# Delta rule in a decoder: one wide product with the block inverse in place of two narrow passes

## The chip, the cores and the metric

The program runs on one NeuronCore of one Trainium2 chip. The metric is the device time of one execution in microseconds; the median of three runs is given. Differences of about 0.3% are what a measurement of this kernel can tell from no change.

## What is computed

The reference is a small decoder of two layers on x of shape (8, 128, 256). The change lies in the attention of the second layer, a gated delta rule with 16 key heads and 32 value heads of width 128. After the projections, a causal convolution over 4 taps and silu, it does this for each of 32 heads and 8 batches:

```python
g = -jnp.exp(A_log) * jax.nn.softplus(a + dt_bias)
gc = jnp.cumsum(gT.reshape(Bs, NV, N, CHUNK), axis=-1)
diff = gc[..., :, None] - gc[..., None, :]
decay = jnp.exp(jnp.where(tril, diff, 0.0)) * tril
A = -(jnp.einsum('bhnid,bhnjd->bhnij', k_beta, kc) * decay) * strict
Tm = jax.scipy.linalg.solve_triangular(eye - A, eye, lower=True, unit_diagonal=True)
u = jnp.einsum('bhnij,bhnjv->bhniv', Tm, v_beta)
...
attn = jnp.einsum('bhid,bhjd->bhij', q_i, k_i) * dec_i
v_new = u_i - jnp.einsum('bhid,bhdv->bhiv', kcd_i, St)
out_i = inter + jnp.einsum('bhij,bhjv->bhiv', attn, v_new)
```

The result is normalised by its root mean square, gated with silu(z) and multiplied by W_out. The kernel takes a sequence of 128 as one chunk, which gives the same numbers: it solves one triangular system of 128 rows for each head and batch, and multiplies the solution by the decayed matrix of queries and keys.

## The kernel before

The program has four phases, one after the other: "a" and "b" are layer 0, "c" is the delta rule, "d" is the rest of layer 1. Names in the profile carry the phase, so `c_NP` is the tile NP of the delta rule. Only phase c is touched.

Phase c works in 8 rounds of 4 value heads (2 key heads) and 8 batches, 32 items of 128x128 each. Rounds 0 to 6 are an iteration of a loop each and prepare the next round inside themselves (`more` is true); round 7 stands behind the loop and prepares nothing. A round does this, in the order written out by hand for each engine:

- SyncE (`gather`) has brought the four 32x32 diagonal blocks of every item's key matrix into the tile A and has cleared them in NP. NP holds for each item two 128x128 matrices side by side: index 0 is N, the decayed key matrix, index 1 is the decayed query matrix, here called Q.
- VectorE inverts the diagonal blocks in 62 steps on the tile T (L1549 to L1553) and then copies T with its indices exchanged into A (L1554). `scatter` on SyncE stores T and A to HBM and loads them as block diagonals into Tb and TbT (L1069 to L1077). Meanwhile TensorE projects the four value chunks (L1172, `c_wv`) and the output gate z (L1232).
- VectorE convolves (L1501), ScalarE applies silu (L1385), TensorE transposes the values (L1221).
- The **products pass**: 32 items Tb x N in `items("MT_ps", ...)`, copied by ScalarE over N, four items of 128 columns in a copy (`c_NP<-c_bank`). The transposes of value chunks 2 and 3 stand between them, each behind the silu of its chunk.
- Three **apply passes** of 32 items: Y = V - M Y, VectorE subtracts (L1566). ScalarE and VectorE prepare the next round's four key and query chunks meanwhile; of each chunk ScalarE makes the square (L1390), whose column sums TensorE takes with a one-column matmul for each batch (`norms`, L1182). VectorE adds a convolution tap after each of the last three subtractions of a pass, and convolves the fourth chunk after the third pass.
- The **W pass**: 32 items TbT x Y, copied by ScalarE back to Y.
- `norms` of the third chunk, then the **C pass**: 32 items Q x W, copied by ScalarE to Y and squared by ScalarE (L1442) and GpSimd (L1131) for the root mean square.
- `norms` of the fourth chunk, then decays and gram matrices of the next round, and the output projection (L1326).

All engines take their instructions in order. PSUM has 8 banks; passes over items take banks 0 to 3 in turn, so group n waits for the copy of group n - 4. A float32 matmul is two hardware instructions with a weight load each, so 32 items are 64 matmuls in the trace.

Of the kernel before, what the change touches and what calls it, by code (L numbers as in the profile page):

```python
# [10 lines left out]
F32 = mybir.dt.float32  # L11
# [7 lines left out]
P = 128  # L19
# [34 lines left out]
class Phase:  # L54
# [5 lines left out]
    def sb(self, name, shape, dt=F32):  # L60
        return self.ctx.enter_context(self.nc.sbuf_tensor(f"{self.tag}_{name}", shape, dt))
# [880 lines left out]
HB = 4  # L942
# [12 lines left out]
def layer1_delta_rule(nc, sems, d, x_src, x_dst):  # L955
# [7 lines left out]
    with ctx:  # L963
# [38 lines left out]
        Tb = sb("Tb", [P, ITEMS, P])  # L1002
        TbT = sb("TbT", [P, ITEMS, P])
        Y = sb("Y", [P, HB, B, S])
# [5 lines left out]
        HALF_ITEMS = ITEMS // KB  # L1010
        blocks = nc.dram_tensor("diagonal_blocks", (3, NBL, ITEMS, BL, BL), F32, kind="Internal").ap()
        no_blocks = nc.dram_tensor("no_blocks", (BL, ITEMS, BL), F32, kind="Internal").ap()
        names = """none_stored blocks_out T_out A_out weights consts pool_step x_loaded xT_ps xT_copied ba_ps gate_step gate_act gc_ps gates_ready
            qk_loaded v_loaded z_loaded out_loaded gates_used proj_ready pad_ready tap0_ready conv_step cv_ready silu_ready sq_ready norms_ps
            root_ready rms_ready csqa_ready norm_step gcrow_ps E_ready GP_ps NP_ready gathered elim_step Tb_placed TbT_placed diag_cleared
            vt_ps V_ready z_ps z_ready MT_ps MT_ready apply_ps y_ready W_ps W_ready C_ps C_ready csq_ready s2_ready
            var_ready f_step y_scaled yT_ps yT_ready out_ps acc_step
            ln_step ln_log ln_rstd xo_ready stored""".split()
        s = {n: sem(n) for n in names}
        quads = [(h, q) for h in range(HB) for q in range(2)]  # L1020
        flat = lambda ap: ap.rearrange("p a b -> p (a b)")
        ELIM = 2 * (BL - 1) + 2
        BLOCKS_OUT = 16 * KB * NBL
# [13 lines left out]
        def _(sp):  # L1037
# [29 lines left out]
            def scatter(i):  # L1067

                sp.wait_ge(s["elim_step"], at(i, ELIM, ELIM - 1))  # L1069
                sp.dma_start(blocks[1].rearrange("r t i j -> (r t) i j"), T[:, :, :]).then_inc(s["T_out"], 16)  # L1070
                sp.wait_ge(s["elim_step"], at(i, ELIM, ELIM))
                sp.dma_start(blocks[2].rearrange("r t i j -> (r t) i j"), A[:, :, :]).then_inc(s["A_out"], 16)
                for n, dst, out, placed in ((1, Tb, "T_out", "Tb_placed"), (2, TbT, "A_out", "TbT_placed")):
                    sp.wait_ge(s[out], at(i, 16, 16))
                    for r in range(NBL):
                        rows = slice(BL * r, BL * r + BL)
                        sp.dma_start(dst[rows, :, rows], blocks[n, r].rearrange("t i j -> i t j")).then_inc(s[placed], 16)  # L1077

# [29 lines left out]
        def _(pool):  # L1108
# [13 lines left out]
            link(pool.memset(Tb[:, :, :], 0.0))  # L1122
            link(pool.memset(TbT[:, :, :], 0.0))
            link(pool.memset(pad[:, :, :, :], 0.0))
# [12 lines left out]
        def _(pe):  # L1137
# [86 lines left out]
            def out_gate(i, b):  # L1224
# [8 lines left out]
                last.then_inc(s["z_ps"], 1)  # L1233

            def items(ps, n, lhsT, rhs):

                h, q = quads[n]
                for b in range(4):
                    last = pe.matmul(banks[n % 4][:, b * P:(b + 1) * P], lhsT(h, 4 * q + b), rhs(h, 4 * q + b), start=True, stop=True)  # L1239
                last.then_inc(s[ps], 1)  # L1240

            def apply(i, rep):

                y = V if rep == 0 else Y
                for n in range(8):
                    if rep == 0:
                        pe.wait_ge(s["MT_ready"], at(i, 8, min(n + 5, 8)))
                    else:
                        pe.wait_ge(s["y_ready"], at(i, 24, 8 * (rep - 1) + n + 1))
                    if n >= 4 or rep:  # L1250
                        pe.wait_ge(s["y_ready"], at(i, 24, 8 * rep + n - 3))
                    items("apply_ps", n, lambda h, b: NP[:, h, b, 0, :], lambda h, b: y[:, h, b, :])
# [7 lines left out]
            def round_(i, more):  # L1260
# [10 lines left out]
                pe.wait_ge(s["pad_ready"], at(i, 2 * CHUNKS, 2 * CHUNKS))  # L1271
                for n in range(8):
                    if n >= 4:
                        pe.wait_ge(s["MT_ready"], at(i, 8, n - 3))
                    items("MT_ps", n, lambda h, b: Tb[:, h * B + b, :], lambda h, b: NP[:, h, b, 0, :])
                    if n == 2:
                        values(i, 2)
                    if n == 6:
                        values(i, 3)
# [11 lines left out]
                if more:  # L1291
                    norms(i + 1, 1)
                pe.wait_ge(s["TbT_placed"], at(i, 16 * NBL, 16 * NBL))
                for n in range(8):
                    pe.wait_ge(s["y_ready"], at(i, 24, 16 + max(n + 1, min(n + 5, 8))))
                    if n >= 4:
                        pe.wait_ge(s["W_ready"], at(i, 8, n - 3))
                    items("W_ps", n, lambda h, b: TbT[:, h * B + b, :], lambda h, b: Y[:, h, b, :])
                if more:
                    norms(i + 1, 2)  # L1300
                for n in range(8):
                    pe.wait_ge(s["W_ready"], at(i, 8, min(n + 5, 8)))
                    if n >= 4:
                        pe.wait_ge(s["C_ready"], at(i, 8, n - 3))
                    items("C_ps", n, lambda h, b: NP[:, h, b, 1, :], lambda h, b: Y[:, h, b, :])
# [38 lines left out]
        def _(act):  # L1344
# [68 lines left out]
            def round_(i, more):  # L1413
# [7 lines left out]
                copy_in(i, QK + 3)  # L1421
                for n, (h, q) in enumerate(quads):
                    if n == 2:
                        silu(i, QK + 2)
                    if n == 3 and more:
                        copy_in(i + 1, 0)
                    if n == 5:
                        silu(i, QK + 3)
                    copy_quad(i, "MT_ps", n, NP[:, h, 4 * q:4 * q + 4, 0, :], "MT_ready")
                if more:  # L1430
# [44 lines left out]
        def _(dve):  # L1475
# [67 lines left out]
            def round_(i, more):  # L1543
# [5 lines left out]
                for j in range(BL - 1):  # L1549
# [600 lines left out]
```

## Time and profile before

| | |
|---|---|
| median of 3 runs | 2425.04 us (2422.2 to 2428.43) |
| the profiled execution | 2429.71 us |
| its span in the profile | 2428.0 us |
| mean granted TensorE clock | 0.891 |
| TensorE matmul busy | 2050.6 us, 84% |
| VectorE busy | 1460.7 us, 60% |
| ScalarE busy | 880.9 us, 36% |
| GpSimd busy | 140.1 us, 6% |

The share of busy time says that TensorE matters most. Matmuls overlap in this count, so a busy TensorE may still have room. What a change is worth is read from the stretch that it touches, instruction by instruction, and from the wait that ends last there.

### The profile page before, as it was taken

To read this page: it belongs to the slowest core of one execution; us is meant where nothing else is said; L and a number is where in the kernel's file an instruction comes from. 1 tells how busy PE (TensorE), PEld (TensorE's weight loads), DVE (VectorE), ACT (ScalarE), POOL (GpSimd) and SP (SyncE) were. 2 spreads that over 40 slices of the span, in tenths; PEclk is the share of its full clock that TensorE was granted. 3 is DMA by queue.
4 is the path that set the end of the run, shared out by engine and by line. 5 is a ranking of instruction groups with operands and counts; after the bars stand their busy time and mean duration, and the time that the engine had idled before them with its cause. 6 is when DMAs were issued, how large, how long until landed. Compare 5 with 4: busy or idle time off the path is not lost. (4 is left out here: it accounts for less than half of the span.)

```text
span 2428.0 us, 30948 instructions
## 1 busy us (share of the span) xinstructions
PE 2050.6 (84%) x10836; PEld 1521.5 (63%) x10850; DVE 1460.7 (60%) x3251; ACT 880.9 (36%) x1542; POOL 140.1 (6%) x130
## 2 busy tenths in 40 slices
PE   6988987998985889898998989989899883787786
PEld 4867776554553568485684856848668582465454
DVE  3557665323222576767767667676676854657666
ACT  2433433111113445443453534535345431333233
POOL 1011010000002000000000000000000001011110
PEclk8889888999996889999999999999999995787787
DMA  3000000400001120301203012030120202000000
GB/s 125 5 13 9 4 5 24 165 1 9 0 9 56 36 53 19 77 9 36 53 19 79 10 36 53 14 81 11 36 53 14 66 1 68 7 11 9 10 4 5
DMA packets 163244, 78.53 MB, mean 32 GB/s; under 512 B 140530, under 2 KB 152628, under 8 KB 162132
## 3 DMA queue, kind: packets, MB, share of 16 engines
q1 hardware_dynamic: 163124, 76.99, 11.7%
q8 instruction: 68, 1.11, 0.2%
q14 instruction: 52, 0.43, 0.1%
HBM read 59.88 MB, written 16.91 MB: 32 GB/s over the span
## 5 line engine op out<-in xcount | busy, mean ns | idle before, releaser
L1566 DVE TENSOR_TENSOR c_Y<-c_V,c_bank 128x512 f32<-128x512 f32 x192 | 131.9, 687 | 82.2 <-PE c_bank L1239 82.2
L1239 PE MATMUL c_bank<-c_Y,c_NP 128*128 128x128 f32 x1536 | 176.4, 276 | 0.0
L1239 PEld LDWEIGHTS c_bank<-c_Y,c_NP 128*128 128x128 f32 x1536 | 173.9, 192 | 3.3 <-issue 3.3
L1540 DVE SCALAR_TENSOR_TENSOR c_NP<-c_NP,c_cj,c_bank 128x256 f32<-128x256 f32 x256 | 104.9, 476 | 68.5 <-ACT c_NP L1410 68.5
L1172 PE MATMUL c_bank<-c_xT,c_wv 128*128 128x512 f32 x256 | 123.1, 643 | 26.9 <-issue 23.3
L1172 PE MATMUL c_bank<-c_xT,c_wqk 128*128 128x512 f32 x256 | 128.6, 650 | 5.1 <-ACT c_pad L1366 3.1
L1501 DVE SCALAR_TENSOR_TENSOR c_cv<-c_pad,c_wcqk,c_cv 128x1024 f32<-128x1024 f32 x96 | 122.2, 1280 | 12.2 <-ACT c_cv L1380 11.4
L1501 DVE SCALAR_TENSOR_TENSOR c_cv<-c_pad,c_wcv,c_cv 128x1024 f32<-128x1024 f32 x96 | 122.5, 1283 | 4.8 <-ACT c_cv L1380 1.6
L1326 PE MATMUL c_bank<-c_wout,c_yT 128*128 128x256 f32 x512 | 121.3, 383 | 0.0
L1366 ACT ACTIVATE c_pad<-c_bank 128x512 f32<-128x512 f32 x128 | 69.0, 592 | 131.7 <-PE c_bank L1172 131.7
L1172 PEld LDWEIGHTS c_bank<-c_xT,c_wv 128*128 128x128 f32 x256 | 52.2, 207 | 94.4 <-issue 94.1
L1232 PE MATMUL c_bank<-c_wz,c_xT 128*128 128x512 f32 x256 | 111.2, 592 | 0.0
L855 ACT ACTIVATE b_sg<-b_G 128x512 f32<-128x512 f32 x50 | 29.8, 597 | 220.6 <-PE b_G L808 220.6
L901 DVE TENSOR_TENSOR b_inner<-b_prod,b_R 128x512 f32<-128x512 f32 x44 | 30.3, 688 | 125.8 <-PE b_R L822 88.2
L1410 ACT ACTIVATE c_NP<-c_bank,c_gcnR 128x128 f32<-128x128 f32 x256 | 73.2, 368 | 84.6 <-PE c_bank L1195 84.5
L1131 POOL TENSOR_TENSOR c_V<-c_Y 128x512 f32<-128x512 f32 x32 | 33.3, 1041 | 1199.5 <-ACT c_Y L1403 1199.5
L1326 PEld LDWEIGHTS c_bank<-c_wout,c_yT 128*128 128x128 f32 x512 | 93.9, 192 | 10.9 <-ACT c_yT L1454 0.2
L808 PE MATMUL b_G<-b_xT,b_wup 128*128 x200 | 97.3, 610 | 2.0 <-ACT b_partsT L858 2.0
L808 PE MATMUL b_U<-b_xT,b_wup 128*128 x200 | 94.6, 595 | 0.0
L832 PE MATMUL b_Y<-b_wdown,b_inner 128*128 128x256 f32 x400 | 93.8, 379 | 0.6
L1552 DVE TENSOR_TENSOR c_tmp<-c_A,c_T 128x31 f32<-128x31 f32 (+15 forms) x248 | 84.9, 342 | 15.0 <-DMA c_A<-diagonal_blocks 6.0
L1385 ACT ACTIVATE c_qkT<-c_cv 128x1024 f32<-128x1024 f32 x32 | 34.0, 1062 | 161.9 <-DVE c_cv L1501 161.9
(409 smaller groups left out, 4262.3 us busy)
## 6 DMA issues: line engine op xcount, KB each, us to landing
b_wup<-b_in_wup SPq DMA_DIRECT2D x4, 1280.0 KB, 14.3
c_wqk<-c_in_wqk SPq DMA_DIRECT2D x9, 512.0 KB, 3.4
c_wv<-c_in_wv SPq DMA_DIRECT2D x8, 512.0 KB, 3.4
c_wz<-c_in_wz SPq DMA_DIRECT2D x8, 512.0 KB, 5.6
c_wout<-c_in_wout SPq DMA_DIRECT2D x8, 512.0 KB, 4.5
diagonal_blocks<-c_NP SPq DMA_DIRECT2D x64, 64.0 KB
c_A<-diagonal_blocks SPq DMA_DIRECT2D x8, 512.0 KB, 3.5
c_NP<-no_blocks SPq DMA_DIRECT2D x32, 128.0 KB, 3.8
```

The costliest lines, as they stand in the source:

```text
L808: last = pe.matmul(bank[:, :], wup[:, t, k, m, :], xT[:, bass.ds(i, 1), m, :].rearrange("p a n -> p (a n)"), start=m == 0, stop=m == DC - 1)
L832: last = pe.matmul(Y[b // 2][:, b % 2 * D:(b % 2 + 1) * D], inner[:, n % 2, b * P:(b + 1) * P], wdown[:, n, :], start=False, stop=n == ECH ...
L1172: last = pe.matmul(four(pair[q][:, :]), w[:, c * P:(c + 1) * P], xT[:, c, 4 * q:4 * q + 4, :], start=c == 0, stop=c == DC - 1)
L1232: last = pe.matmul(banks[6 + b % 2][:, :], xT[:, c, b, :], wz[:, c, :], start=c == 0, stop=c == DC - 1)
L1239: last = pe.matmul(banks[n % 4][:, b * P:(b + 1) * P], lhsT(h, 4 * q + b), rhs(h, 4 * q + b), start=True, stop=True)
L1326: last = pe.matmul(banks[2 + m % 2][:, 0:D], yT[:, m % 2, h, :], wout[:, h, :], start=h == 0, stop=h == HB - 1)
L1366: act.activation(pad[:, m % 2, 4 * q:4 * q + 4, TAPS - 1:], four(pair[q][:, :]), ACT.Copy)\
L1410: act.activation(NP[:, h, 4 * q + b, 1, :], banks[4 + n % 2][:, b * P:(b + 1) * P], ACT.Exp, bias=gcnR[:, h, 4 * q + b:4 * q + b + 1]).the ...
L1501: dve.scalar_tensor_tensor(cv[:, m % 2], pad[:, m % 2, :, t:t + S], w, cv[:, m % 2], ALU.mult, ALU.add)\
L1540: dve.scalar_tensor_tensor(NP[:, h, bb, :, :], spread(NP[:, h, bb, 1, :], 2), cj[:, h, bb:bb + 1], gp, ALU.mult, ALU.mult).then_inc(s["NP_ ...
L1552: elim(dve.tensor_tensor(part, along(A[:, j, j + 1:BL], w), spread(T[:, j, 0:w], n), ALU.mult))
L1566: dve.tensor_tensor(rr(Y, h, q), rr(V, h, q), four(banks[n % 4][:, :]), ALU.subtract).then_inc(s["y_ready"], 1)
```

## The change

N and Q of an item lie side by side in NP. The changed kernel multiplies both by the block inverse in one matmul of 256 columns, Tb x [N Q], and copies both products back over NP. The C pass then takes Y itself, since (Tb Q) transposed times Y is what Q transposed times the W pass's result was. The W pass, its copies, the tile TbT, its memset on GpSimd, the exchanged copy of T on VectorE and five DMAs of `scatter` go. In `products` a unit is two items in one bank; 16 units with a copy of 512 columns each take the place of 8 groups of four items. The C pass waits for the third pass's subtractions (`y_ready`) as the W pass did. `silu(i + 1, 3)` of ScalarE moves from between the W copies to behind the second C copy.

```diff
-                sp.wait_ge(s["elim_step"], at(i, ELIM, ELIM))
-                sp.dma_start(blocks[2].rearrange("r t i j -> (r t) i j"), A[:, :, :]).then_inc(s["A_out"], 16)
-                for n, dst, out, placed in ((1, Tb, "T_out", "Tb_placed"), (2, TbT, "A_out", "TbT_placed")):
...
-            link(pool.memset(TbT[:, :, :], 0.0))
...
+            def products(i, u):
+
+                h, b0 = units[u]
+                if u >= 4:
+                    pe.wait_ge(s["MT_ready"], at(i, UNITS, u - 3))
+                for b in range(2):
+                    last = pe.matmul(banks[u % 4][:, b * 2 * P:(b + 1) * 2 * P], Tb[:, h * B + b0 + b, :],
+                                     NP[:, h, b0 + b, :, :].rearrange("p a n -> p (a n)"), start=True, stop=True)
+                last.then_inc(s["MT_ps"], 1)
...
-                for n in range(8):
-                    if n >= 4:
-                        pe.wait_ge(s["MT_ready"], at(i, 8, n - 3))
-                    items("MT_ps", n, lambda h, b: Tb[:, h * B + b, :], lambda h, b: NP[:, h, b, 0, :])
-                    if n == 2:
+                for u in range(UNITS):
+                    products(i, u)
+                    if u == 5:
                         values(i, 2)
-                    if n == 6:
+                    if u == 13:
                         values(i, 3)
...
                 apply(i, 2)
                 if more:
                     norms(i + 1, 1)
-                pe.wait_ge(s["TbT_placed"], at(i, 16 * NBL, 16 * NBL))
-                for n in range(8):
-                    pe.wait_ge(s["y_ready"], at(i, 24, 16 + max(n + 1, min(n + 5, 8))))
-                    if n >= 4:
-                        pe.wait_ge(s["W_ready"], at(i, 8, n - 3))
-                    items("W_ps", n, lambda h, b: TbT[:, h * B + b, :], lambda h, b: Y[:, h, b, :])
                 if more:
                     norms(i + 1, 2)
                 for n in range(8):
-                    pe.wait_ge(s["W_ready"], at(i, 8, min(n + 5, 8)))
+                    pe.wait_ge(s["y_ready"], at(i, 24, 16 + max(n + 1, min(n + 5, 8))))
...
-                for n, (h, q) in enumerate(quads):
-                    if n == 2:
+                for u, (h, b0) in enumerate(units):
+                    if u == 4:
                         silu(i, QK + 2)
-                    if n == 3 and more:
+                    if u == 6 and more:
                         copy_in(i + 1, 0)
-                    if n == 5:
+                    if u == 10:
                         silu(i, QK + 3)
-                    copy_quad(i, "MT_ps", n, NP[:, h, 4 * q:4 * q + 4, 0, :], "MT_ready")
+                    act.wait_ge(s["MT_ps"], at(i, UNITS, u + 1))
+                    act.activation(NP[:, h, b0:b0 + 2, :, :].rearrange("p b a n -> p (b a n)"), banks[u % 4][:, :], ACT.Copy)\
+                        .then_inc(s["MT_ready"], 1)
...
                 for n, (h, q) in enumerate(quads):
-                    if more and n == 5:
+                    if more and n == 2:
                         silu(i + 1, 3)
-                    copy_quad(i, "W_ps", n, rr(Y, h, q), "W_ready")
-                for n, (h, q) in enumerate(quads):
...
-                elim(dve.tensor_copy(A[:, :, :], T[:, :, :].rearrange("p i k -> p k i")))
```

TensorE in the loop, products pass, before: `c_ident,c_cv` is the transpose of a value chunk, `c_wqk` a projection of the next round.

```order
L1172 MATMUL c_bank<-c_xT,c_wqk 128x512 x4
L1269 ISA
L1239 MATMUL c_bank<-c_NP,c_Tb 128x128 x12
L1214 REGISTER_ALU
L1221 MATMUL c_bank<-c_ident,c_cv 128x128 x8
L1239 MATMUL c_bank<-c_NP,c_Tb 128x128 x16
L1214 REGISTER_ALU
L1221 MATMUL c_bank<-c_ident,c_cv 128x128 x8
L1239 MATMUL c_bank<-c_NP,c_Tb 128x128 x4
```

The same place in the changed kernel, up to the first transposes and one unit further.

```order
L1169 MATMUL c_bank<-c_xT,c_wqk 128x512 x4
L1276 ISA
L1238 MATMUL c_bank<-c_NP,c_Tb 128x256 x8
L1236 REGISTER_ALU
L1238 MATMUL c_bank<-c_NP,c_Tb 128x256 x2
L1236 REGISTER_ALU
L1238 MATMUL c_bank<-c_NP,c_Tb 128x256 x2
L1211 REGISTER_ALU
L1218 MATMUL c_bank<-c_ident,c_cv 128x128 x8
```

The transposes of chunk 2 stood behind 12 items and stand behind 12 wide items now.

TensorE in the loop, from the last group of the third apply pass to the norms of the fourth chunk, before (`c_ones,c_sq` are the norms).

```order
L1239 MATMUL c_bank<-c_Y,c_NP 128x128 x4
L1180 REGISTER_ALU
L1182 MATMUL c_bank<-c_ones,c_sq 128x1 x8
L1295 REGISTER_ALU
L1239 MATMUL c_bank<-c_Y,c_TbT 128x128 x4
L1295 REGISTER_ALU
L1239 MATMUL c_bank<-c_Y,c_TbT 128x128 x4
L1295 REGISTER_ALU
L1239 MATMUL c_bank<-c_Y,c_TbT 128x128 x4
L1295 REGISTER_ALU
L1239 MATMUL c_bank<-c_Y,c_TbT 128x128 x20
L1180 REGISTER_ALU
```

The same place in the changed kernel.

```order
L1246 MATMUL c_bank<-c_Y,c_NP 128x128 x4
L1177 REGISTER_ALU
L1179 MATMUL c_bank<-c_ones,c_sq 128x1 x8
L1177 REGISTER_ALU
L1179 MATMUL c_bank<-c_ones,c_sq 128x1 x8
L1301 REGISTER_ALU
L1246 MATMUL c_bank<-c_Y,c_NP 128x128 x4
L1301 REGISTER_ALU
```

Between the norms of chunk 1 and those of chunk 2 stood the 32 items of the W pass; nothing stands there now.

## Rows read from the trace of the kernel before

**Rows 1.** Windows, round 2: us, busy of PE, PEld, DVE, ACT, POOL, granted clock, DMA.

```profile
1132.20:1284.60 152.40, 136.96 (x776) 104.17 (x776) 105.87 (x217) 68.26 (x117) 4.16 (x4) 0.96 0.17 39
```

**Rows 2.** Timeline, products pass of round 2: start us, us, engine, line, operation, [idle before <-releaser].

```profile
1174.81 2.84 PE L1239 MATMUL c_bank<-c_NP,c_Tb 128*128 128x128 f32 x24
...
1178.39 1.09 PE L1221 MATMUL c_bank<-c_ident,c_cv 128*128 128x128 f32 x8 [0.74 <-ACT c_cv L1385]
...
1179.91 1.15 ACT L1380 ACTIVATE c_cv<-c_pad,c_wcqk 128x1024 f32<-128x1024 f32 x1
...
1185.16 3.67 PE L1172 MATMUL c_bank<-c_xT,c_wqk 128*128 128x512 f32 x8
```

**Rows 3.** Timeline and page groups: TensorE's pace at full clock, 256 and 128 columns.

```profile
1123.87 3.62 PE L1326 MATMUL c_bank<-c_wout,c_yT 128*128 128x256 f32 x16
...
1188.67 7.31 PE L1239 MATMUL c_bank<-c_V,c_NP 128*128 128x128 f32 x64
...
L1326 PE MATMUL c_bank<-c_wout,c_yT 128*128 128x256 f32 x512 | 121.3, 383 | 0.0
...
L1239 PE MATMUL c_bank<-c_Y,c_TbT 128*128 128x128 f32 x512 | 60.7, 277 | 8.7 <-ACT c_Y L1403 8.7
```

**Rows 4.** Timeline of round 2, from the norms of chunk 1 to those of chunk 3.

```profile
1218.65 1.87 PEld L1182 LDWEIGHTS c_bank<-c_ones,c_sq 128*128 128x128 f32 x16
...
1221.37 5.12 DVE L1501 SCALAR_TENSOR_TENSOR c_cv<-c_pad,c_wcqk,c_cv 128x1024 f32<-128x1024 f32 x4
...
1223.85 1.06 ACT L1390 ACTIVATE c_sq<-c_qkT 128x1024 f32<-128x1024 f32 x1
...
1225.53 3.81 PE L1239 MATMUL c_bank<-c_Y,c_TbT 128*128 128x128 f32 x32 [1.25 <-ACT c_Y L1403]
...
1227.20 1.08 ACT L1385 ACTIVATE c_qkT<-c_cv 128x1024 f32<-128x1024 f32 x1
...
1229.36 1.55 ACT L1403 ACTIVATE c_Y<-c_bank 128x512 f32<-128x512 f32 x3
...
1230.88 7.39 PE L1239 MATMUL c_bank<-c_Y,c_NP 128*128 128x128 f32 x64
...
1232.06 0.60 ACT L1403 ACTIVATE c_Y<-c_bank 128x512 f32<-128x512 f32 x1 [1.15 <-PE c_bank L1239]
...
1237.69 1.22 ACT L1403 ACTIVATE c_Y<-c_bank 128x512 f32<-128x512 f32 x2
...
1239.14 1.94 PE L1182 MATMUL c_bank<-c_ones,c_sq 128*128 128x1 f32 x16 [0.87 <-ACT c_Y L1403]
```

**Rows 5.** Windows around falls of TensorE's granted clock, columns as in rows 1.

```profile
1128.60:1132.00 3.40, 0.00 (x0) 0.00 (x0) 0.00 (x0) 0.00 (x0) 0.00 (x0) 0.99 0.46 152
1132.00:1138.80 6.80, 5.53 (x7) 2.44 (x8) 5.98 (x20) 0.00 (x0) 0.00 (x0) 0.50 0.03 6
1237.80:1241.20 3.40, 2.53 (x23) 2.32 (x22) 2.75 (x7) 3.06 (x5) 1.04 (x1) 1.00 0.00 0
...
934.00:940.80 6.80, 6.80 (x28) 6.08 (x29) 2.40 (x12) 3.18 (x8) 0.00 (x0) 0.50 0.00 0
```

**Rows 6.** Timeline of the weight loads: norms in a stretch at half clock, ahead of round 0.

```profile
788.99 3.49 PEld L1182 LDWEIGHTS c_bank<-c_ones,c_sq 128*128 128x128 f32 x16 [0.36 <-ACT c_sq L1390]
```

**Rows 7.** Timeline of round 1: the exchanged copy, and the first silu behind it.

```profile
1004.77 1.04 DVE L1554 COPY c_A<-c_T 128x1024 f32<-128x1024 f32 x1
...
1009.90 1.06 ACT L1385 ACTIVATE c_cv<-c_cv 128x1024 f32<-128x1024 f32 x1 [4.54 <-DVE c_cv L1501]
```

**Rows 8.** Timeline and DMA issues at the start of phase c.

```profile
730.73 0.43 SPq L1040 DMA_DIRECT2D c_acc<-x_after_b x1
...
737.99 3.51 POOL L1123 MEMSET c_TbT<- 128x4096 f32 x1
...
743.61 3.67 PE L1143 MATMUL c_bank<-c_ident,c_acc 128*128 128x128 f32 x16 [25.10 <-POOL c_ones L1125]
...
c_acc<-x_after_b SPq DMA_DIRECT2D x1, 1024.0 KB, 5.7
```

More of the change, by code:

```diff
@@ L1002, in layer1_delta_rule @@
         Tb = sb("Tb", [P, ITEMS, P])
-        TbT = sb("TbT", [P, ITEMS, P])
         Y = sb("Y", [P, HB, B, S])
@@ L1010, in layer1_delta_rule @@
         HALF_ITEMS = ITEMS // KB
-        blocks = nc.dram_tensor("diagonal_blocks", (3, NBL, ITEMS, BL, BL), F32, kind="Internal").ap()
+        blocks = nc.dram_tensor("diagonal_blocks", (2, NBL, ITEMS, BL, BL), F32, kind="Internal").ap()
         no_blocks = nc.dram_tensor("no_blocks", (BL, ITEMS, BL), F32, kind="Internal").ap()
-        names = """none_stored blocks_out T_out A_out weights consts pool_step x_loaded xT_ps xT_copied ba_ps gate_step gate_act gc_ps gates_ready
+        names = """none_stored blocks_out T_out weights consts pool_step x_loaded xT_ps xT_copied ba_ps gate_step gate_act gc_ps gates_ready
             qk_loaded v_loaded z_loaded out_loaded gates_used proj_ready pad_ready tap0_ready conv_step cv_ready silu_ready sq_ready norms_ps
-            root_ready rms_ready csqa_ready norm_step gcrow_ps E_ready GP_ps NP_ready gathered elim_step Tb_placed TbT_placed diag_cleared
-            vt_ps V_ready z_ps z_ready MT_ps MT_ready apply_ps y_ready W_ps W_ready C_ps C_ready csq_ready s2_ready
+            root_ready rms_ready csqa_ready norm_step gcrow_ps E_ready GP_ps NP_ready gathered elim_step Tb_placed diag_cleared
+            vt_ps V_ready z_ps z_ready MT_ps MT_ready apply_ps y_ready C_ps C_ready csq_ready s2_ready
             var_ready f_step y_scaled yT_ps yT_ready out_ps acc_step
@@ L1020, in layer1_delta_rule @@
         quads = [(h, q) for h in range(HB) for q in range(2)]
+        units = [(h, 2 * u) for h in range(HB) for u in range(B // 2)]
+        UNITS = len(units)
         flat = lambda ap: ap.rearrange("p a b -> p (a b)")
-        ELIM = 2 * (BL - 1) + 2
+        ELIM = 2 * (BL - 1) + 1
         BLOCKS_OUT = 16 * KB * NBL
@@ L1067, in scatter @@
             def scatter(i):
-                sp.wait_ge(s["elim_step"], at(i, ELIM, ELIM - 1))
+                sp.wait_ge(s["elim_step"], at(i, ELIM, ELIM))
                 sp.dma_start(blocks[1].rearrange("r t i j -> (r t) i j"), T[:, :, :]).then_inc(s["T_out"], 16)
-                sp.wait_ge(s["elim_step"], at(i, ELIM, ELIM))
-                sp.dma_start(blocks[2].rearrange("r t i j -> (r t) i j"), A[:, :, :]).then_inc(s["A_out"], 16)
-                for n, dst, out, placed in ((1, Tb, "T_out", "Tb_placed"), (2, TbT, "A_out", "TbT_placed")):
[L1074 to L1077, printed above, removed]
+                sp.wait_ge(s["T_out"], at(i, 16, 16))
+                for r in range(NBL):
+                    rows = slice(BL * r, BL * r + BL)
+                    sp.dma_start(Tb[rows, :, rows], blocks[1, r].rearrange("t i j -> i t j")).then_inc(s["Tb_placed"], 16)
             load_qk(0)
@@ L1246, in apply @@
                     if rep == 0:
-                        pe.wait_ge(s["MT_ready"], at(i, 8, min(n + 5, 8)))
+                        pe.wait_ge(s["MT_ready"], at(i, UNITS, min(UNITS - 3 + n, UNITS)))
                     else:
```

## Prediction

> **What bounds the kernel now.** The page's busy shares say TensorE, so I looked at one loop round. In round 2, TensorE is busy for 136.96 of 152.40 us at a mean clock of 0.96, VectorE for 105.87 [rows 1]. That is near a bound, but the time is lost or won at the waits, so I read the timeline of the two stretches that the change touches. In the products pass TensorE works almost throughout: it starts at 1174.81, waits 0.74 us for the silu of chunk 2, and the projection behind the pass starts at 1185.16, so the stretch lasts 10.35 us [rows 2]. The second stretch runs from the norms of chunk 1 at 1218.65 to the norms of chunk 3 at 1239.14, 20.5 us [rows 4]. In it, TensorE waits 1.25 us in the middle of the W pass for a copy that stands behind a silu, and 0.87 us at the end. Everything else in it is covered, and by what is the question here: the norms of chunk 2 come behind the W pass.
>
> **Products pass.** First the paces at full clock. A chain of n matmuls lasts n - 1 paces and one instruction's own time: for 256 columns (3.62 - 0.38) / 15 = 0.216 us, for 128 columns (7.31 - 0.28) / 63 = 0.112 us [rows 3]. The pass had 64 narrow matmuls, 7.15 us, and has 64 wide ones, 13.8 us. Behind units 5 and 13 stand 8 transposes each, 0.9 us a time. ScalarE must copy 16 units at 0.6, do two silus of 1.06, and one copy-in of 2 x 0.55 + 1.15 us [rows 2, 4], together 14.0 us, under the 15.6 us of TensorE, so TensorE sets the pace. I walked the two queues against each other: the silu of chunk 2 stands behind the copy of unit 3, and ends 0.2 us after TensorE is done with unit 5; no other wait is left. The 0.74 us wait goes, since the six wide units cover that silu. The stretch is then 13.8 + 1.8 + 0.2 = 15.8 us instead of 10.35: **+5.5 us**. The two narrow paces that a wide one replaces are 0.224 against 0.216, so joining the passes saves TensorE 0.5 us a round and no more.
>
> The Trainium skill ("Perfetto Trace Analysis", Optimizing Tensor Performance, Matmuls) says that larger matmuls are more efficient than smaller ones. The trace agrees only by that 4%, so nothing of the sum changes by it.
>
> **W pass.** Its 7.15 us on TensorE go, the 1.25 us wait inside it too. But the norms of chunk 2 now follow those of chunk 1 directly, and they need the square that ScalarE starts at 1223.85 and ends at 1224.9. It hangs on the third pass's last tap on VectorE, which the change doesn't move. TensorE is done with the norms of chunk 1 at 1220.5 and stands still for 4.5 us; it had worked on W then. Behind it in its queue waits the whole C pass. At full clock: norms 1225.0 to 1226.8, C from 1226.8 instead of 1230.88. ScalarE copies group 0 of C 1.1 us after it begins (1232.06 against 1230.88) and group 1 0.9 us later, squares for 0.5, and starts the silu of chunk 3 at 1230.0, where VectorE's four taps (done at 1226.5) no longer hold it. From that silu to the next copy it takes 2.16 us (1227.20 to 1229.36), so copy 2 starts at 1232.1, and each pair of copies with its square 1.78 us after the last. The last pair starts at 1235.7; before, it started at 1237.69. So the stretch is 2.0 us shorter, not 7: ScalarE's order ends it. All of it rests on [rows 4].
>
> **The clock.** From 1218.65 to the C pass TensorE would do only one-column matmuls and 4.5 us of nothing. In the rows, 3.4 us without any matmul at the end of a round are followed by 6.8 us at 0.50, that is 1.2 GHz instead of 2.4, and that although work began again early in these 6.8 us. The clock has also fallen after 3.4 us with the end of C, the 0.87 us gap and the norms, with busy 2.53 of 3.4; at this place of round 0 it then stays at 0.50 for 6.8 us [rows 5]. So norms don't hold the clock up, and I expect it to have fallen before the norms of chunk 2 begin. Then their 16 weight loads take 3.49 us instead of 1.87, +1.6 [rows 4, 6], and the first two groups of C, on which copy 1 and everything behind it on ScalarE hang, take 1.8 instead of 0.9 us each, +1.8. Later groups have room, since copy 2 waits for silu and square anyway. The stretch is then 2.0 - 3.4 = **1.4 us longer**. Behind it, TensorE idles some 2.5 us instead of 0.87 before the norms of chunk 3, so the fall of the clock at this place [rows 5] comes sooner or lasts longer. Bounds: 0 and 3.3 us (norms at half clock 1.6, and half of 3.4 us more); I take **+1.0**, nearer to 0, as ScalarE and VectorE set much of what follows.
>
> **The rest.** The exchanged copy of T costs VectorE 1.04 us. In round 1 ScalarE waits 4.54 us for the convolution behind it [rows 7]; rounds 0, 1 and 5 have this wait, the others find VectorE early. So -1.06 x 3 = **-3.2 us**, and nothing in rounds 2, 3, 4 and 6, where TensorE's work covers it. The five DMAs of `scatter` are on SyncE ahead of weight loads that nobody waits for: 0. In round 7 there are no norms between the passes: products +5.9 (no copy-in), W pass -7.15, the copy of T -0.4: **-1.7 us**. At the start of the phase TensorE waits for GpSimd's last constant, and the 3.51 us memset of TbT is in that chain; the DMA of x, issued at 730.73, has landed 5.7 us later, at 736.4, ahead of the new start near 740.0. So **-3.6 us** [rows 8].
>
> **Sum.** Seven loop rounds: 7 x (5.5 + 1.4 + 1.0) = +55.3. With -3.2, -1.7 and -3.6: **+47 us**. The profiled execution took 2429.7 us, which gives 2476.5. It is 4.7 us above the median of the runs, 2425.0, so I predict 2472 us for the median, 1.9% slower.
>
> **Rivals.** (1) The clock holds through the stall, or falls so late that the C pass hardly feels it. The rows don't show a fall with norms on both sides of a gap, which speaks for it; the fall at 1241.2 with much less idle time speaks against. Then 7 x (5.5 - 2.0) - 8.5 = +16, 2441 us. The Trainium skill ("TensorE: Matmul & The Clock Gate", What's actually happening) makes the low clock the default that activity lifts; by that this rival loses. No run yet shows the case.
>
> (2) The end of a round: all engines do nothing for 3.4 us there [rows 5], and in four of the rounds 2 to 6 TensorE's next matmul comes some 5 us after its last wait ends, with no releaser. TensorE's program is 128 instructions shorter in a round, so this could go. It is worth at most 3.4 x 4 = 14 us: +33 with the low clock, 2458; +2 with the full one, 2427, no change.
>
> (3) Faster: the square of chunk 2 is done when the third pass ends, so there is no stall. Then the C pass begins near 1222.3, the silu of chunk 3 waits for VectorE at 1226.5, and the last pair of copies comes 5.5 us sooner than before: a loop round gains nothing and loses nothing, and 8.5 us remain, 2416.5. It decides from a stall of under 0.3 us; each us more costs each loop round one, up to 3.5. Against it: VectorE's last tap of that pass stands behind its last subtraction, which stands behind TensorE's own matmuls.
>
> (4) Heavier: the clock costs its upper bound behind C too, 7 x 10.2 - 8.5 = +63, 2488 us.
>
> **Chances.** Forecast 0.66, rival 1 0.18, rival 2 0.10, half of it no change, rival 3 0.02, rival 4 0.04. A difference under 0.3%, some 7 us, can't be told from none. Faster by more: rival 3 and a little, 0.03. Within: half of rival 2 and the low edge of rival 1, 0.07. Slower: 0.90. The range reaches from rival 1's lower side, 2436, to rival 4, 2488; below lie most of rival 2 and part of rival 1.
>
> **What would show it.** From the norms of chunk 1 to C a gap of 4 to 5 us on TensorE that ends with ScalarE's square (c_sq), in 7 rounds. The granted clock at 0.50 over the norms of chunk 2 and the start of C, their 16 weight loads at 3.4 us. Products stretch 15.8 us; norms of chunk 1 to norms of chunk 3 21.9 us at the low clock, 18.5 at the full one. TensorE's first matmul of the phase 3.6 us sooner. I would be wrong if the gap is covered, if the wide matmuls go at another pace than 0.216 us, or if the rounds' ends change length.

## The result, and the profile after

The changed kernel takes **2440.97 us** (2438.44 to 2443.09, 4 runs), the kernel before 2426.4 us (2422.2 to 2428.43, 4 runs): a ratio of 1.0061, 95% interval 1.0046 to 1.0076. It is slower, as forecast, and inside the range, but by 14.6 us and not by 47. The profiled executions took 2441.95 and 2429.71 us, and their spans differ by 12.2 us. The ledger below is made against that.

First the head of the page and three of its groups, after. Behind the last bar of a group stands the idle time of the engine ahead of it, and what ended it.

```profile
span 2440.2 us, 30017 instructions
...
PE 2055.9 (84%) x10338; PEld 1521.5 (62%) x10338; DVE 1451.5 (59%) x3243; ACT 882.6 (36%) x1542; POOL 136.4 (6%) x129
...
q8 instruction: 31, 0.51, 0.1%
...
L1169 PE MATMUL c_bank<-c_xT,c_wv 128*128 128x512 f32 x256 | 111.8, 594 | 7.8 <-DVE c_acc L1592 7.3
L1238 PE MATMUL c_bank<-c_NP,c_Tb 128*128 128x256 f32 x512 | 116.1, 383 | 0.0
L1179 PE MATMUL c_bank<-c_ones,c_sq 128*128 128x1 f32 x512 | 75.8, 278 | 44.1 <-ACT c_sq L1389 31.3
```

The busy shares say nothing: TensorE's is 84% as before. The groups say two things. The norms have 31.3 us of waits for c_sq ahead of them, 4.4 us in each of seven rounds: the stall that the prediction named. And the projection that opens a round (c_wv) waits 7.3 us in all for the residual. The page of the kernel before has these two lines in the same places:

```profile
q8 instruction: 68, 1.11, 0.2%
...
L1172 PE MATMUL c_bank<-c_xT,c_wv 128*128 128x512 f32 x256 | 123.1, 643 | 26.9 <-issue 23.3
```

There, 23.3 us of the wait had no releaser ("issue"), and the queue q8 of kind "instruction" moved 68 packets of 16 KB instead of 31. This is where the forecast went wrong.

**The stretches that the prediction spoke of**, in round 2. First the products pass, timeline after, columns as in [rows 2]:

```profile
1174.42 5.34 PE L1238 MATMUL c_bank<-c_NP,c_Tb 128*128 128x256 f32 x24
...
1180.60 7.07 PE L1238 MATMUL c_bank<-c_NP,c_Tb 128*128 128x256 f32 x32
...
1190.11 1.45 PE L1169 MATMUL c_bank<-c_xT,c_wqk 128*128 128x512 f32 x3
```

From 1174.42 to 1190.11 are 15.7 us; before it was 10.35 [rows 2]. 32 wide matmuls last 7.07, that is (7.07 - 0.38) / 31 = 0.216 us a pace, as taken from [rows 3]; no wait for ScalarE is left. Next, the stretch of [rows 4], norms of chunk 1 to norms of chunk 3:

```profile
1223.63 1.84 PE L1179 MATMUL c_bank<-c_ones,c_sq 128*128 128x1 f32 x16
...
1228.72 1.06 ACT L1389 ACTIVATE c_sq<-c_qkT 128x1024 f32<-128x1024 f32 x1
1229.83 3.49 PEld L1179 LDWEIGHTS c_bank<-c_ones,c_sq 128*128 128x128 f32 x16 [4.43 <-ACT c_sq L1389]
...
1233.27 7.06 PE L1246 MATMUL c_bank<-c_Y,c_NP 128*128 128x128 f32 x48
...
1240.79 2.02 PE L1246 MATMUL c_bank<-c_Y,c_NP 128*128 128x128 f32 x16 [0.46 <-ACT c_Y L1402]
...
1244.64 1.94 PE L1179 MATMUL c_bank<-c_ones,c_sq 128*128 128x1 f32 x16 [1.82 <-ACT c_Y L1402]
```

TensorE stands still for 4.4 us until ScalarE's square is done, and then the 16 weight loads of the norms take 3.49 us, the figure of half clock in [rows 6]. The windows show the clock (us, busy of PE, PEld, DVE, ACT, POOL, granted clock, DMA):

```profile
1226.10:1236.30 10.20, 6.47 (x30) 6.47 (x31) 5.48 (x8) 2.71 (x3) 0.27 (x1) 0.50 0.19 52
1243.20:1246.60 3.40, 1.96 (x17) 1.97 (x18) 2.79 (x6) 3.11 (x5) 1.23 (x2) 1.00 0.00 0
1246.60:1250.00 3.40, 3.40 (x13) 2.91 (x13) 1.84 (x10) 2.85 (x7) 0.00 (x0) 0.50 0.00 0
```

The clock is at 0.50, 1.2 GHz, for 10.2 us, from 0.6 us into the stall on, as forecast. The fall behind the norms of chunk 3 lasts 3.4 us, no longer than the one at 1241.2 before. The window of it in the kernel before:

```profile
1241.20:1244.60 3.40, 3.40 (x14) 2.85 (x13) 1.77 (x9) 2.77 (x7) 0.00 (x0) 0.50 0.00 0
```

**The ledger**, stretch by stretch over all rounds, read from the two timelines as differences of starts (the norms of a chunk are its 16 one-column matmuls):

| stretch | predicted | before | after | measured |
|---|---|---|---|---|
| first products matmul to norms of chunk 1, 7 rounds | +38.5 | 43.96 each | 49.22 each | +36.8 |
| norms of chunk 1 to norms of chunk 3, 7 rounds | +9.8 | 20.39 each | 21.28 (round 2: 21.00) | +6.0 |
| norms of chunk 3 to the next products, 7 times, and the way to the first products | +3.4 | 86.20 to 89.30; into round 7 77.88; first 124.76 | 83.87 to 86.46; 75.15; 124.26 | -22.6 |
| rest of round 7 | -1.3 | 73.26 | 70.96 | -2.3 |
| start of the phase, and all behind it | -3.6 | first matmul at 743.61 | at 738.70 | -5.7 |
| sum | +47 | | | +12.2 |

Most of the miss, 26 of some 35 us, lies in one line, between the norms of chunk 3 and the next round's products. The lengths of that stretch, from round 1 to round 6, were 88.91, 88.84, 89.30, 89.02, 86.20, 88.83 and are 86.46, 84.01, 85.85, 85.77, 83.87, 85.79. At the start of round 2, the timeline of TensorE shows what went, first before and then after:

```profile
1123.87 3.62 PE L1326 MATMUL c_bank<-c_wout,c_yT 128*128 128x256 f32 x16
1133.27 1.19 PE L1172 MATMUL c_bank<-c_xT,c_wv 128*128 128x512 f32 x1 [5.79 <-issue]
```

```profile
1128.33 3.62 PE L1325 MATMUL c_bank<-c_wout,c_yT 128*128 128x256 f32 x16
1133.02 13.97 PE L1169 MATMUL c_bank<-c_xT,c_wv 128*128 128x512 f32 x32 [1.07 <-DVE c_acc L1592]
```

Measured from VectorE's last addition to the residual, on which the matmul waits, the gap was 0.68, 5.33, 5.81, 5.29, 0.70 and 5.01 us in rounds 1 to 6. It is 0.61 to 0.66 in all of them now.

### The profile page after: what moved, and what is told of

It reads as the page before. It is cut to its first block and busy times, and to the rows that moved or that the text cites. A ratio compares the mean times of both kernels' runs of the same rounds, so it can differ in the third digit from the quotient of the medians.

```text
span 2440.2 us, 30017 instructions
## 1 busy us (share of the span) xinstructions
PE 2055.9 (84%) x10338; PEld 1521.5 (62%) x10338; DVE 1451.5 (59%) x3243; ACT 882.6 (36%) x1542; POOL 136.4 (6%) x129
## 5 line engine op out<-in xcount | busy, mean ns | idle before, releaser
L1246 PE MATMUL c_bank<-c_Y,c_NP 128*128 128x128 f32 x1536 | 191.3, 288 | 1.7 <-ACT c_Y L1402 1.7
L1246 PEld LDWEIGHTS c_bank<-c_Y,c_NP 128*128 128x128 f32 x1536 | 188.1, 204 | 6.1 <-issue 5.9
L1500 DVE SCALAR_TENSOR_TENSOR c_cv<-c_pad,c_wcqk,c_cv 128x1024 f32<-128x1024 f32 x96 | 122.2, 1280 | 12.2 <-ACT c_cv L1379 11.5
L1169 PE MATMUL c_bank<-c_xT,c_wv 128*128 128x512 f32 x256 | 111.8, 594 | 7.8 <-DVE c_acc L1592 7.3
L1238 PE MATMUL c_bank<-c_NP,c_Tb 128*128 128x256 f32 x512 | 116.1, 383 | 0.0
L1179 PE MATMUL c_bank<-c_ones,c_sq 128*128 128x1 f32 x512 | 75.8, 278 | 44.1 <-ACT c_sq L1389 31.3
L1238 PEld LDWEIGHTS c_bank<-c_NP,c_Tb 128*128 128x128 f32 x512 | 97.2, 193 | 15.8 <-issue 3.3
L1179 PEld LDWEIGHTS c_bank<-c_ones,c_sq 128*128 128x128 f32 x512 | 75.5, 232 | 50.1 <-ACT c_sq L1389 32.1
L1128 POOL TENSOR_TENSOR c_V<-c_Y 128x512 f32<-128x512 f32 x32 | 33.2, 1039 | 1218.3 <-ACT c_Y L1402 1218.3
L1325 PEld LDWEIGHTS c_bank<-c_wout,c_yT 128*128 128x128 f32 x512 | 93.4, 191 | 10.6 <-ACT c_yT L1453 0.2
L1218 PE MATMUL c_bank<-c_ident,c_cv 128*128 128x128 f32 x256 | 47.6, 346 | 56.4 <-ACT c_cv L1384 56.4
```

Of the source, the lines that this page charges most:

```text
L1169: last = pe.matmul(four(pair[q][:, :]), w[:, c * P:(c + 1) * P], xT[:, c, 4 * q:4 * q + 4, :], start=c == 0, stop=c == DC - 1)
L1179: last = pe.matmul(banks[7][:, m * B + b:m * B + b + 1], sq[:, m % 2, b, :], ones[:, :], start=True, stop=True)
L1238: last = pe.matmul(banks[u % 4][:, b * 2 * P:(b + 1) * 2 * P], Tb[:, h * B + b0 + b, :], NP[:, h, b0 + b, :, :].rearrange("p a n -> p (a n ...
L1325: last = pe.matmul(banks[2 + m % 2][:, 0:D], yT[:, m % 2, h, :], wout[:, h, :], start=h == 0, stop=h == HB - 1)
L1500: dve.scalar_tensor_tensor(cv[:, m % 2], pad[:, m % 2, :, t:t + S], w, cv[:, m % 2], ALU.mult, ALU.add)\
```

## Experiments

Theory: the stretches inside a round went as forecast (stall, fall of the clock), and the shorter code of TensorE's loop body took away a reload of code at the start of each iteration. Rivals: the gap at the round's start depends on where the code lies, or on something else that the change removed (the buffer, its DMAs, the copy); and the stall alone, not the clock, is what the W stretch costs.

### Is it the length of the loop's code?

In the trace TensorE runs 1638 instructions in each loop round before (776 matmuls, 776 weight loads, 86 register, semaphore and branch instructions) and 1519 after (712, 712 and 95), counted from one round's opening projection to the next round's. This is the length of the loop's body. One kernel puts the length back, and one shortens the old kernel.

tiny64, the changed kernel with 64 one-column matmuls (128 instructions) in the stall, where TensorE has nothing to do:

```diff
                 if more:
+                    pe.wait_ge(s["y_ready"], at(i, 24, 21))
+                    for _ in range(64):
+                        pe.matmul(banks[0][0:32, 0:1], identb[:, 0:32], identb[:, 0:1], start=True, stop=True)
                     norms(i + 1, 2)
```

> The changed kernel with 64 matmuls of one column (128 hardware instructions, some 3 us) in the stall between the norms of chunk 1 and those of chunk 2, so the loop's code on TensorE is as long as in the kernel before. Theory (the loop's code is kept when short enough and fetched again when longer, and that fetch made the 5 us gap at the end of four rounds before): 16 KB instruction packets in most rounds, TensorE's first matmul of the next round some 5 us behind its last wait instead of 0.6, time 10 to 18 us longer, 2455. Rival (the gap went because SyncE has five DMAs less, or because the rounds' ends fall otherwise against its traffic): no packets, gap 0.6, 2441.

Measured: 2460.39 us (2456.57 to 2462.88), ratio to before 1.0138 [1.0103, 1.0172]. The stretch with the stall keeps its length (21.03 to 21.28 us), so the 64 matmuls cost nothing there. Its page, the queue's line and the opening projection's group, and the timeline at the start of round 2:

```profile
q8 instruction: 86, 1.41, 0.2%
...
L1169 PE MATMUL c_bank<-c_xT,c_wv 128*128 128x512 f32 x256 | 125.5, 653 | 35.3 <-issue 34.0
```

```profile
1128.94 3.62 PE L1328 MATMUL c_bank<-c_wout,c_yT 128*128 128x256 f32 x16
1138.50 7.88 PE L1169 MATMUL c_bank<-c_xT,c_wv 128*128 128x512 f32 x14 [5.94 <-issue]
```

The gap is back, in all six rounds and not in four (34.0 us for 6 of them), with 9 packets of 16 KB in each. From the norms of chunk 3 to the next products the six rounds take 17.4 us more than in the changed kernel.

before_short, the kernel before with its norms by one matmul a chunk, 112 instructions less; it leaves out the norms of batches 1 to 7, which get the value of batch 0:

```diff
-                for b in range(B):
-                    last = pe.matmul(banks[7][:, m * B + b:m * B + b + 1], sq[:, m % 2, b, :], ones[:, :], start=True, stop=True)
+                last = pe.matmul(banks[7][:, m * B:m * B + B], sq[:, m % 2, 0, :], ones[:, :].broadcast_to([P, B]), start=True, stop=True)
```

> The kernel before with each norms of 8 batches made with one matmul instead of 8 (the norms of batches 1 to 7 are left out, they get the value of batch 0), so the loop's code on TensorE is 112 instructions shorter, about as long as in the changed kernel; W pass, scatter and all else as before. Theory of the code's length: no 16 KB instruction packets between rounds 1 and 7, TensorE's gap at the round's end 0.6 us in every round. The time falls by some 2 us in each of 4 rounds for the gap, and by up to 7 x 3 us for the norms themselves: 2400 to 2420. Rival (SyncE's DMAs): gaps of 5 us stay in most rounds.

Measured: 2389.25 us (2383.74 to 2391.19), ratio 0.9842 [0.9807, 0.9878]. The old kernel with its W pass, its copy and its buffer loses the gap as well (0.61 to 0.63 us in every round):

```profile
q8 instruction: 31, 0.51, 0.1%
...
L1172 PE MATMUL c_bank<-c_xT,c_wv 128*128 128x512 f32 x256 | 111.8, 594 | 7.7 <-DVE c_acc L1593 7.3
```

So neither the buffer nor its DMAs nor the copy made the gap. Of its 37 us, most are the norms themselves, which are left out in part. The six stretches into the next products are 24.2 us shorter; some 9.6 of these I put down to the shorter norms in them (7 in 8 matmuls of one set, 1.6 us a round), which is an estimate. Not all of the other 14.6 is the gap: rounds 1 and 5, which had none, are 5.6 us shorter, 3.2 by the norms, and have less half clock. The four rounds that lost the gap are 18.6 us shorter, 6.4 by the norms, so 12.2 remain for the gap and the half clock that came with it.

Where is the step, and is it length or place? The same 64 matmuls stand ahead of the loop in tiny64_ahead, so the body is as short as the changed kernel's but lies elsewhere:

```diff
+            for _ in range(64):
+                pe.matmul(banks[0][0:32, 0:1], identb[:, 0:32], identb[:, 0:1], start=True, stop=True)
             with pe.Fori(0, ROUNDS - 1) as i:
                 round_(i, True)
```

> Control for the code's length: the same 64 one-column matmuls (128 instructions), once ahead of the loop instead of inside it, so each round's code is as long as the changed kernel's but stands elsewhere in memory. Theory: the loop's length decides, so 0 packets of 16 KB in rounds 2 to 6, gap 0.6, and 2441 us plus at most 4 for the 64 matmuls once. Rival: where the code lies decides (a boundary it crosses), then 8 to 9 packets a round and a gap of 5 us come back, 2459.

Measured: 2441.22 us (2438.34 to 2445.3), ratio 1.0053 [1.0037, 1.0069], as the changed kernel. 31 packets, no gap. tiny16 and tiny32 are tiny64 with `range(16)` and `range(32)`:

> The changed kernel with 16 one-column bf16 matmuls (32 instructions) in TensorE's stall before the norms of chunk 2; computes the same. Theory: what the 64 tiny matmuls cost was a step that comes with the length of the loop's code (the changed kernel's round shows 0 instruction packets of 16 KB and a gap of 0.61 to 0.66 us before TensorE's first matmul of a round, the 64 gave 9 packets and some 5 us). With 32 instructions more the loop is still shorter than the old kernel's, so either nothing happens (0 packets, gap 0.6, 2441 us) or the whole step (8 to 9 packets a round, gap about 5, some +18 us, 2459). Rival: the cost is in proportion to the instructions added, 19.4 us for 128, so +5 us, 2446, with a gap between 0.6 and 5.

> The same with 32 one-column matmuls (64 instructions). Theory of a step: 0 packets, gap 0.6 and 2441 us, or 8 to 9 packets, gap about 5 and 2459; never before the run with 16 shows it too. Rival, in proportion: +10 us, 2451.

Measured: tiny16 2441.1 us (2437.31 to 2443.74), ratio 1.0049 [1.0032, 1.0066]; tiny32 2445.6 us (2440.64 to 2450.46), ratio 1.0071 [1.005, 1.0093]. The queue's line and the opening projection's, on the page of tiny16 and then on that of tiny32:

```profile
q8 instruction: 31, 0.51, 0.1%
...
L1169 PE MATMUL c_bank<-c_xT,c_wv 128*128 128x512 f32 x256 | 111.8, 594 | 7.7 <-DVE c_acc L1595 7.3
```

```profile
q8 instruction: 58, 0.95, 0.2%
...
L1169 PE MATMUL c_bank<-c_xT,c_wv 128*128 128x512 f32 x256 | 117.8, 620 | 21.5 <-issue 16.9
```

By the profile, one iteration of the loop refetches, with 9 packets, or it passes without one. The table goes by one profiled execution of each kernel:

| kernel | instructions of TensorE in the body | rounds with the gap, of 1 to 6 | packets of 16 KB on the page |
|---|---|---|---|
| after, tiny64_ahead | 1519 | 0 | 31 |
| before_short | 1526 | 0 | 31 |
| tiny16 | 1551 | 0 | 31 |
| tiny32 | 1583 | 3 (1, 3, 4) | 58 |
| before | 1638 | 4 (2, 3, 4, 6) | 68 |
| tiny64 | 1647 | 6 | 86 |

The rival that cost grows with each instruction falls with tiny16: 32 more are free, and no round shows a part of the gap. A clean step it is not either. At 1583 and at 1638 instructions a kernel has the gap in some rounds and not in others, and my expectation for tiny32, all or nothing, missed that: 2445.6 us lies between the two times I gave. Its seven runs spread from 2440.6 to 2450.5 us, so the number of such rounds may differ between executions; one alone was traced. What decides in one round of tiny32 or of before stays open.

The Trainium skill ("Runtime: NRT & Kernel Launch", Instruction fetch mechanics) says that a taken branch whose target isn't in the current window forces a fetch of it before execution goes on. The trace agrees for the long bodies: the gap stands at the loop's start alone. Of the 9 packets of such a round, 3 or 4 come from 8 us before its first matmul to 5 us behind it, and the others are spread over the round. For the short bodies the trace shows another thing: rounds 1 to 6 of the changed kernel pass without one packet of 16 KB, so the whole body was still there. The same goes for rounds 1 and 5 of the kernel before.

### Stall and clock

norms_late puts the norms of chunk 2 behind the fourth group of the C pass, so that TensorE works on C while ScalarE makes the square:

```diff
-                if more:
-                    norms(i + 1, 2)
                 for n in range(8):
                     ...
                     items("C_ps", n, lambda h, b: NP[:, h, b, 1, :], lambda h, b: Y[:, h, b, :])
+                    if more and n == 3:
+                        norms(i + 1, 2)
```

> The changed kernel with one edit: the norms of chunk 2 stand behind the fourth group of the C pass instead of ahead of it. Theory (the stall of TensorE for ScalarE's square costs, and the fall of the clock behind it): the C pass begins right behind the norms of chunk 1, ScalarE's copies begin when its square of chunk 2 is done, norms of chunk 1 to norms of chunk 3 lasts 15 us instead of 21.3, the clock does not fall there, and the time is 7 x 6.2 = 43 us shorter, 2398 us. Rival (ScalarE's queue alone ends this stretch, the stall is cover): the stretch stays near 20 us and the time near 2435.

Measured: **2395.71 us** (2390.07 to 2397.19), ratio 0.9866 [0.9832, 0.9901]. It computes the same and is faster than both kernels. TensorE's timeline of the stretch in round 2, and a window over it:

```profile
1210.29 1.84 PE L1179 MATMUL c_bank<-c_ones,c_sq 128*128 128x1 f32 x16
1212.00 3.82 PE L1246 MATMUL c_bank<-c_Y,c_NP 128*128 128x128 f32 x32
1216.49 1.95 PE L1179 MATMUL c_bank<-c_ones,c_sq 128*128 128x1 f32 x16 [0.67 <-ACT c_sq L1389]
1218.30 2.03 PE L1246 MATMUL c_bank<-c_Y,c_NP 128*128 128x128 f32 x16
1220.90 2.02 PE L1246 MATMUL c_bank<-c_Y,c_NP 128*128 128x128 f32 x16 [0.58 <-ACT c_Y L1402]
```

```profile
1209.00:1224.00 15.00, 12.68 (x110) 12.13 (x108) 13.01 (x17) 9.47 (x15) 4.00 (x3) 1.00 0.12 36
```

The stretch is 14.46 us long instead of 21.28 (15.95 in round 6, where the clock fell for 6.8 us), and of the 4.4 us stall 0.67 is left. The seven stretches are 46 us shorter together, the time 45. The stall and what followed from it were worth more than the whole change had cost.

How much of it is the clock? filler keeps the order, and runs 16 matmuls of 512 bf16 columns inside the stall, whose result nobody reads:

```diff
                 if more:
+                    pe.wait_ge(s["y_ready"], at(i, 24, 21))
+                    for _ in range(16):
+                        pe.matmul(banks[0][:, :], identb[:, :], spread(hiddenb[:, :], 4), start=True, stop=True)
+                if more:
                     norms(i + 1, 2)
```

> The changed kernel with 16 bf16 matmuls of 512 columns into bank 0 (3.4 us at full clock, their result is overwritten by the C pass) in the stall between the norms of chunk 1 and those of chunk 2. The stall is still waited out, only the array is busy in it. Theory (the half clock costs): granted clock 1.00 through the C pass, the 16 weight loads of the norms 1.9 us, norms of chunk 1 to norms of chunk 3 18.5 us instead of 21.3, 20 us less in all, 2421. Rival (the half clock is hidden behind ScalarE's queue): 2441.

Measured: 2425.27 us (2418.82 to 2438.18, 10 runs), ratio 0.999 [0.9969, 1.0012], 16 us below the changed kernel. The profiled execution was the longest of them, 2438.18, and shows rounds with and without the fall of the clock. Round 1, and the window over its stretch:

```profile
1062.09 1.84 PE L1179 MATMUL c_bank<-c_ones,c_sq 128*128 128x1 f32 x16
1063.80 3.61 PE L1301 MATMUL c_bank<-c_hiddenb,c_identb 128*128 128x512 bf16 x16
1068.29 1.95 PE L1179 MATMUL c_bank<-c_ones,c_sq 128*128 128x1 f32 x16 [0.88 <-ACT c_sq L1393]
1070.10 5.61 PE L1246 MATMUL c_bank<-c_Y,c_NP 128*128 128x128 f32 x48
```

```profile
1062.09:1080.01 17.92, 14.76 (x114) 12.26 (x113) 11.71 (x17) 10.32 (x16) 3.76 (x4) 1.00 0.11 30
```

With the clock up, the stretch is 17.92 us (rounds 0 and 1), against 21.28: the clock is worth 3.4 us a round here, the sum of the two items of 1.6 and 1.8 us in the prediction. In the other rounds of this execution it fell for 3.4 us (18.5 us long) or for 6.8 us (20.2) all the same. What the seven stretches gained, 15.2 us, was in good part lost behind them: the stretches into the next products took 10.6 us more than in the changed kernel, with 98 us at half clock instead of 79. So this execution was only 3.8 us faster than the profiled one of the changed kernel, and where the 16 us of the median come from was not traced. Matmuls that do nothing can give back the clock, but not in every round, while work moved into the stall gives back stall and clock.

### The exchanged copy and the memset

copy_memset_back puts two removed pieces of work back into the changed kernel, with results that nobody reads:

```diff
                 elim.close()
+                dve.wait_ge(s["gates_used"], at(i, 3, 3))
+                dve.tensor_copy(A[:, :, :], T[:, :, :].rearrange("p i k -> p k i"))
...
             link(pool.memset(Tb[:, :, :], 0.0))
+            link(pool.memset(Y[:, :, :, :], 0.0))
```

> The changed kernel with the exchanged copy of T on VectorE at a round's start and a 3.51 us memset on GpSimd among the constants put back; both write what nothing reads. Theory: with the gap of 5 us gone from the rounds' ends every loop round now waits for VectorE at its start, so the copy costs 1.06 us in all of rounds 0 to 6, not in three of them, +7.4 us, and the memset +3.6: 2452 us. Rival, as the prediction had it: the copy costs 1.06 in rounds 0, 1 and 5 alone, +3.2, and the memset +3.6: 2448 us. In the trace: norms of chunk 3 to the next products pass 1.06 us longer in each round, first matmul of the phase 3.5 us later.

Measured: 2456.6 us (2452.89 to 2457.9), ratio 1.0121 [1.0087, 1.0154]; 15.4 us above tiny64_ahead, which ran beside it and is as fast as the changed kernel. In round 2, from VectorE's cast at the round's start to TensorE's transposes of the values, first after and then with the copy:

```profile
1135.12 0.68 DVE L1546 CAST c_T<-c_T 128x1024 f32<-128x1024 bf16 x1
...
1164.57 1.71 PE L1218 MATMUL c_bank<-c_ident,c_cv 128*128 128x128 f32 x7 [3.84 <-ACT c_cv L1384]
```

```profile
1138.55 0.69 DVE L1547 CAST c_T<-c_T 128x1024 f32<-128x1024 bf16 x1
...
1168.93 1.33 PE L1219 MATMUL c_bank<-c_ident,c_cv 128*128 128x128 f32 x5 [6.46 <-ACT c_cv L1385]
```

29.45 and 30.38 us. In rounds 1 to 6 of the changed kernel this distance is 29.43 to 29.46, with the copy 30.38 to 30.42. So every loop round now waits for VectorE at this place, and the copy is on the path in all of them; before, it was 30.5 in rounds 1 and 5, and 33.2 to 34.5 in the four with the gap. There the silu ahead of these transposes stands on ScalarE behind its last copy of z (L1399), and that waits for TensorE, which is late. The memset: TensorE's wait for the constants at the start of the phase, after and with the memset back:

```profile
738.70 3.68 PE L1140 MATMUL c_bank<-c_ident,c_acc 128*128 128x128 f32 x16 [21.52 <-POOL c_ones L1122]
```

```profile
745.11 2.18 PE L1141 MATMUL c_bank<-c_ident,c_acc 128*128 128x128 f32 x9 [25.09 <-POOL c_ones L1123]
```

25.09 - 21.52 = 3.57 us. The two are 7 x 0.97 + 3.6 = 10.4 us together. The times show 15.4, 5 more than that; the profiled execution, the shortest of its runs, is 10.9 us longer than the profiled one of the changed kernel. The rest was not traced, and the time alone doesn't tell the two theories (2452 and 2448) apart; the distances in the trace do.

## Why the prediction was right and wrong

- **Products pass, +5.5 a round: right.** Stretch 15.7 us for 15.8 forecast, pace 0.216 us, no wait left. To the norms of chunk 1 it is +5.26. The page shows no idle time ahead of the wide matmuls (0.0), so nothing waited for the DMAs of `scatter`, which the prediction priced at 0.
- **The stall: right.** 4.5 us forecast, 4.4 measured, released by the square.
- **The clock over the norms and C: right,** rival 1 is out. That its 2441 us is the measured time is luck: it left out the fall of the clock, which came, and kept the gaps, which went. The weight loads of the norms take 3.49 us. The stretch is 0.9 us longer instead of 1.4, and with the clock up 17.92 us (filler) instead of 18.5: ScalarE's order behind the start of C gives back half a microsecond more than I had walked out.
- **The clock behind C, +1.0 a round: wrong.** The prediction let the wider gap ahead of the norms of chunk 3 (1.82 instead of 0.87 us) bring a sooner or longer fall. Before, the clock fell behind these norms in all seven rounds, for 6.8 us in round 0 and for 3.4 in the others; after, it fell for 3.4 us in five rounds and not at all in rounds 4 and 6. Rounds 1 and 5, which had no gap at their start, became 2.45 and 2.33 us shorter in the stretch that holds it. The copy is 1.0 of these. For the other 1.3 to 1.4 there is one thing in the records that goes with them: 3.4 us less at half clock in this stretch (17.1 to 13.7 us in round 1, 13.7 to 10.2 in round 5), and it is missing at this very place. Why the clock falls less often there was not tested.
- **The round's start, taken as unchanged: wrong, and the step that failed.** The prediction saw the gap of some 5 us with no releaser, saw 128 matmul and weight instructions fewer (119 in all by the count above), wrote down a rival of 14 us and gave it 0.10. It was right in size: rounds 2, 3, 4 and 6 became 4.83, 3.45, 3.25 and 3.04 us shorter, 14.6 in all, the copy included. tiny64, before_short and tiny64_ahead show that the body's length decides. The prediction did not ask the one question that would have weighed it: how many packets of 16 KB the instruction queue moved in each round (9 with the gap, none without). With that, a gap that code causes and a change that shortens the code make the rival the likelier case.
- **The exchanged copy, -3.2 in three rounds: half right.** It was covered in the four rounds where TensorE was late from the gap. With the gap gone it would have been on the path in all seven, so its removal belongs with the gap's. Two terms that I had summed apart are one.
- **Round 7, -1.7:** -2.3 from its products on, and -2.7 ahead of them. The copy explains 0.4 there by the prediction, 0.45 to 0.56 by the distance of cast and values (29.71 us, 30.16 with the copy back, 30.27 before). Most of the rest, 1.7 us, lies ahead of the cast, where the clock no longer falls behind the norms of chunk 3. That is no steady gain: the same stretch takes 75.15 us in tiny16 as well, and 76.8 in tiny32, tiny64, tiny64_ahead and norms_late, without any difference in round 7's code.
- **Memset, -3.6: right.** The wait is 3.57 us shorter. The phase began 4.9 us sooner in the profile; the other 1.3 lie ahead of the wait, and over the seven profiled kernels without the memset, in which nothing ahead of the phase differs, its start lies between 737.08 and 741.97.

The two errors, 1.0 a round behind C and the rounds' starts, make 26 us of the miss; the products and W stretches together 5.5, the ends of the phase 3.

## What to carry to other kernels

Where an engine idles at a loop's start with no releaser, count the instruction queue's packets there: if they come with the gap, the body was too long to stay loaded here, and every edit of that engine's program is priced by its length too. When a pass goes, ask which wait it hid (here the next chunk's square), and give that wait other work of the same engine before you judge the edit: the same change cost 0.6% with the norms where they stood and gained 1.3% with them four groups later.

## What the runs showed of the hardware

- TensorE's loop body runs rounds 1 to 6 without a packet of 16 KB at 1551 instructions, refetches in 3 of 6 rounds at 1583, in 4 of 6 at 1638, and in all at 1647. A refetch is 9 packets over the round and a gap of about 5 us at its start, 4.4 more than without. The clock falls with it: the opening projection takes 125.5 us on the page of tiny64 and 111.8 on that of the changed kernel, 2.3 us a round. Of these 6.7 us the transposes of the values feel 4.0 on the mean (32.7 to 34.6 us behind VectorE's cast in tiny64, 29.4 in the changed kernel), since their wait of 3.84 us shrinks (to 1.71 in round 2). At the next products 17.4 / 6 = 2.9 us a round are left.
- One-column norms on both sides of a stall of 4.4 us don't hold the clock up. It fell in all seven rounds, for 10.2 us. The Trainium skill ("TensorE: Matmul & The Clock Gate", What's actually happening) makes the low clock the default that activity lifts, which fits the low clock over the stall. Sixteen real matmuls in the stall kept it up in two of seven rounds of the execution that was profiled.
- The clock makes equal rounds unequal. In the stretch from the norms of chunk 3 to the next products of the changed kernel, the rounds with 10.2 us at half clock take 83.9 to 84.0 us, those with 13.7 us take 85.8 to 86.5. So 2 us more or less in one round of one trace is no evidence for an edit.
